# AFNO blocks on one core: the Filter's mixing as 64x64 tiles, two units at once, and softshrink split between VectorE and ScalarE

## The reference

```python
def afno_filter(x, w1, b1, w2, b2):          # x: 2 x 128 x 128 x 128
    xf = rfft2(x, axes=(1, 2), norm='ortho') # 65 columns kept
    xf = xf.reshape(B, H, W // 2 + 1, 8, 16) # 8 blocks of 16 channels
    o1r = relu(xr @ w1[0] - xi @ w1[1] + b1[0])   # per block
    o1i = relu(xi @ w1[0] + xr @ w1[1] + b1[1])
    o2r = softshrink(o1r @ w2[0] - o1i @ w2[1] + b2[0], 0.01)
    o2i = softshrink(o1i @ w2[0] + o1r @ w2[1] + b2[1], 0.01)
    return irfft2(o2r + 1j * o2i) + x

h = afno_filter(layer_norm(x) * n1_g + n1_b, ...) + x
y = gelu(layer_norm(h) @ mw1 + mb1) @ mw2 + mb2 + h
```

## Time and profile before

| | |
|---|---|
| median of 3 runs | 1652.82 us (1651.64 to 1653.29) |
| the profiled execution | 1653.2 us, its span 1651.4 us |
| TensorE busy, granted clock | 1598.6 us (97%), 1.000 |
| VectorE busy | 1076.1 us (65%) |
| ScalarE busy | 938.4 us (57%) |
| GpSimd busy | 619.8 us (38%) |

### The profile page before, as it was taken

The page is one execution under the profiler, slowest core; times in us unless marked ns, Lnnn a source line. Parts: engine busy times, 40 slices in busy tenths (PEclk is TensorE's granted clock), DMA queues, the critical chain, the costliest instruction groups (busy, mean ns, idle before and its releaser), DMA issues.

```text
span 1651.4 us, 34968 instructions
## 1 busy us (share of the span) xinstructions
PE 1598.6 (97%) x11278; PEld 1445.4 (88%) x11278; DVE 1076.1 (65%) x2697; ACT 938.4 (57%) x1782; POOL 619.8 (38%) x774
## 2 busy tenths in 40 slices
PE   0999999999999999999999999999999999999999
PEld 0999988888999988888899998888889998888888
DVE  7889566556559856655656966665664995555453
ACT  5655276666535546666644545666663553666665
POOL 4800046766800016676660002677673000211111
PEclk9999999999999999999999999999999999999999
DMA  7500713333300062333320042333331006011111
GB/s 222 197 15 1 238 45 108 95 102 121 97 14 1 8 236 83 108 95 102 122 78 1 1 166 94 101 108 101 102 110 46 1 1 204 27 32 38 32 39 45
DMA packets 167249, 137.67 MB, mean 83 GB/s; under 512 B 9459, under 2 KB 131189, under 8 KB 167157
## 3 DMA queue, kind: packets, MB, share of 16 engines
q1 hardware_dynamic: 166354, 136.23, 26.1%
q10 hardware_dynamic: 802, 0.21, 0.1%
HBM read 69.29 MB, written 67.11 MB: 83 GB/s over the span
## 4 chain that ended last, share of the span: by engine, by line
PE 79%; DVE 14%; issue 4%; ACT 1%; SPq 1%; DVEq 1%; DMA 1%; POOL 0%; ACTq 0%
PE ps L756 27%; PE ps L558 7%; PE ps L722 7%; PE ps L724 7%; PE ps L683 7%; PE ps L723 7%; DVE vsb L1105 4%; PE ps L716 3%; PE ps L702 3%; PE ps L708 3%; DVE csb L1107 3%; DVE usb L1095 3%; DVE usb L1096 2%; PE ps L568 2%; PE ps L612 2%
## 5 line engine op out<-in xcount | busy, mean ns | idle before, releaser
L756 PEld LDWEIGHTS ps<-mw,gel 128*128 128x128 f32 x4000 | 520.6, 191 | 42.3
L756 PE MATMUL ps<-mw,gel 128*128 128x128 f32 x4000 | 523.7, 274 | 0.0
L875 ACT ACTIVATE gel<-ps,mb1f 128x512 f32<-128x512 f32 x500 | 343.7, 687 | 250.5 <-PE ps L724 219.7
L1460 POOL TENSOR_TENSOR arena<-arena,mb2rep 128x512 f32<-128x512 f32 x125 | 160.1, 1281 | 654.6 <-ACT hn L861 654.6
L722 PE MATMUL ps<-hth,mw1h 128*128 128x512 f32 x512 | 260.3, 508 | 2.9 <-DVE htl L1206 1.5
L1449 POOL TENSOR_SCALAR arena<-xnext,rstd,shift 128x128 f32<-128x128 f32 x360 | 159.3, 462 | 207.6 <-DVE shift L1344 207.6
L861 ACT ACTIVATE hn<-arena,shift,rstd 128x128 f32 (+1 forms) x512 | 221.7, 483 | 16.7 <-DVE shift L1344 16.7
L1189 DVE TENSOR_TENSOR arena<-ps,arena 128x512 f32 (+1 forms) x60 | 41.5, 691 | 252.4 <-PE ps L708 233.8
L724 PE MATMUL ps<-hth,mw1l 128*128 128x512 f32 x512 | 202.1, 395 | 0.0
L723 PE MATMUL ps<-htl,mw1h 128*128 128x512 f32 x512 | 200.8, 392 | 0.0
L846 ACT ACTIVATE osb<-usb,vectors 128x512 f32<-128x512 f32 (+1 forms) x136 | 95.6, 703 | 158.3 <-DVE usb L1096 158.3
(11 more groups left out here) (118 smaller groups left out, 2397.9 us busy)
## 6 DMA issues: line engine op xcount, KB each, us to landing
arena<-aside SPq DMA_DIRECT2D x128, 256.0 KB, 5.0
aside<-gz SPq DMA_DIRECT2D x96, 256.0 KB, 3.0
between<-xout SPq DMA_DIRECT2D x62, 256.0 KB, 2.3
out_dram<-xout SPq DMA_DIRECT2D x62, 256.0 KB, 2.3
xnext<-between SPq DMA_DIRECT2D x60, 256.0 KB, 3.1
aside<-first SPq DMA_DIRECT2D x32, 256.0 KB, 2.3
xnext<-in_x_dram SPq DMA_DIRECT2D x30, 256.0 KB, 3.1
first<-in_x_dram SPq DMA_DIRECT2D x1, 960.0 KB, 7.2
```

What stands on the lines that cost most here:

```text
L756: mm = pe.matmul(ps[:, r % 2, P * i:P * i + P], gel[:, r % 2, m, P * i:P * i + P], mw2[:, s // IMAGES, m, :], start=(m == 0 and i == 0), s ...
L875: act.activation(gel[:, r % 2, m, :], ps[:, 2 + m % 2], ACT.Gelu, bias=mb1f[:, s // IMAGES, m:m + 1]).then_inc(gelu_out, 1)
L1460: pool.tensor_tensor(t, t, b, ALU.add).then_inc(mb2_done, 1)
```

## The change

The mixing works on two units at once, called a pair `p` (units 2p and 2p+1). Each half of 64 channels is cut once more into quarters of 32 channels (QUART), so that real and imaginary part of a quarter fill 64 partitions. `w1s` and `w2s` become 64x64 blocks. A pair's first mixing is 4 matmuls for the even and 4 for the odd part, one in each 64x64 tile of the array. Its second mixing is 16 matmuls with a 64x128 stationary operand, in the upper and the lower half of the array by turns, and writes to two banks per pair, in pairs of banks that alternate. The biases in `b2cols` are raised by LAM, and softshrink becomes min(v, 0) + relu(v - 2 LAM): VectorE adds the bias (`biased`, L1155), ScalarE applies the rectifier (`upper`, L889), VectorE takes the minimum and the sum in one operation (`shrink`, L1172). TensorE's, ScalarE's and VectorE's programs are written in another order for it. The weights come in 12 transfers and the vectors in 4, in place of 3 and 1; for the first layer the vectors move to SyncE's queue, behind the constants. The Nyquist column is no longer copied to a place of its own.

The core of the diff:

```diff
-            def mix2(s, n):
-                q, kws = n % 2, 1 if n in (2, 3) else GROUP
-                pe.wait_ge(o_out, UNITS * s + n + 1)
-                if n >= 2:
-                    pe.wait_ge(v_out, UNITS * s + n - 1)
-                for i in range(kws):
-                    mm = pe.matmul(ps[:, 4 + q, P * i:P * i + P], osb[:, q, i, :],
-                                   w2s[:, q].rearrange("p r c -> p (r c)"), start=True, stop=True)
-                mm.then_inc(m2_mm, 1)
+            def mix1(s, p):
+
+                alone = p == 1
                 if not alone:
-                    pe.wait_ge(g_out, 2 * BATCHES * s + g + 1)
-                if n >= 2:
-                    pe.wait_ge(u_out, UNITS * s + n - 1)
+                    pe.wait_ge(g_out, 2 * BATCHES * s + spectrum_of(2 * p + 1) + 1)
+                if p:
+                    pe.wait_ge(u_out, UNITS * s + 2 * p)
+
+                def quarters(j0, j1, depth, k0, k1, kind, start):
+
+                    for q in range(2):
+                        for g in range(2):
+                            own_rows = slice(HALF * g + depth[0], HALF * g + depth[1])
+                            cols = slice(HALF * (g ^ q), HALF * (g ^ q) + HALF)
...
+                            mm = pe.matmul(dst[:, :, k0:k1], w1s[own_rows, kind, q].rearrange("p r c -> p (r c)"),
+                                           gsb[own_rows, q, j0:j1, k0:k1], start=start, stop=True, skip_group_check=True)
+                    return mm
...
+                elif p:
+                    quarters(0, GROUP, (0, HALF), 0, EVEN, 0, True)
+                    mm = quarters(0, GROUP, (0, HALF), EVEN, P, 1, False)
...
+                mm.then_inc(m1_mm, 2)
+
+            def mix2(s, p):
+                kws = 1 if p == 1 else GROUP
+                if p >= 2:
+                    pe.wait_ge(v_out, UNITS * s + 2 * p - 2)
+                for q in range(2):
+                    pe.wait_ge(o_out, UNITS * s + 2 * p + q + 1)
+                    for i in range(kws):
+                        for g in range(2):
+                            own_rows = slice(HALF * g, HALF * (g + 1))
+                            at_ = 2 * HALF * 2 * q + HALF * i
+                            mm = pe.matmul(ps[:, 4 + 2 * (p % 2) + g, at_:at_ + HALF], osb[own_rows, q, i, :],
+                                           w2s[own_rows, q].rearrange("p r c -> p (r c)"), start=True, stop=True)
+                mm.then_inc(m2_mm, 2)
...
+                for q in range(2):
+                    dft_h(s, 4 + q)
+                for p in range(PAIRED):
+                    if p + 1 < PAIRED:
+                        mix1(s, p + 1)
+                    if p == EDGE_PAIR + 1:
+                        pe.wait_ge(y_done, (UNITS + 1) * s + 2 * EDGE_PAIR + 2)
+                    mix2(s, p)
+                    if p == EDGE_PAIR:
                         edges(s)
+                    if p and p + 2 < PAIRED:
+                        for q in range(2):
+                            dft_h(s, 2 * p + 4 + q)
...
+            def upper(s, n, q, kws=GROUP):
+                act.wait_ge(v_out, UNITS * s + n + 1)
+                act.activation(csb[:, q, :, 0:kws], vsb[:, q, :, 0:kws], ACT.Relu, bias=cut[:, :]).then_inc(c_out, 1)
...
                 def batch(b, last=False):
                     n = 2 * b + 2
-                    g_copy(s, n + 1, 1)
-                    e_copy(s, n, 0)
+                    for q in range(2):
+                        e_copy(s, n + q, q)
                     o_relu(s, n, 0)
-                    if not last:
-                        g_copy(s, n + 2, 0)
-                    e_copy(s, n + 1, 1)
+                    for q in range(2):
+                        upper(s, n - 2 + q, q, kws=1 if isinstance(b, int) and b == 1 else GROUP)
+                        if not last:
+                            g_copy(s, n + 2 + q, q)
                     o_relu(s, n + 1, 1)
...
+            def biased(s, n, q, odd, kws=GROUP):
...
+                dve.tensor_tensor(v, src, bias, ALU.add).then_inc(v_out, 1)
+
             def shrink(s, n, b, q, kws=GROUP):
 
-                dve.wait_ge(m2_mm, UNITS * s + n + 1)
...
-                dve.tensor_tensor(v, src, bias, ALU.add).then_inc(v_out, 1)
-                dve.wait_ge(v_out, UNITS * s + n + 1)
-                own.add(dve.tensor_scalar(cl, v, -LAM, LAM, ALU.max, ALU.min))
-                own.settle()
...
-                dve.tensor_tensor(dst, v, cl, ALU.subtract).then_inc(y_done, 1)
+                dve.scalar_tensor_tensor(dst, v, 0.0, cl, ALU.min, ALU.add).then_inc(y_done, 1)
...
+                def batch(b, odd, last=False):
+                    if not last:
+                        combine(s, 2 * b + 4, 0)
                     for q in range(2):
-                        if not (last and q):
-                            combine(s, 2 * b + 3 + q, 1 - q)
+                        biased(s, 2 * b + 2 + q, q, odd)
+                    if not last:
+                        combine(s, 2 * b + 5, 1)
+                    for q in range(2):
                         shrink(s, 2 * b + 2 + q, b, q)
...
+            load_weights(act, params[0])
```

More of the change, by code:

```diff
@@ L207, in afno @@
         mask = cst[:, 7 * P:].rearrange("p (s b) -> p s b", s=3)
[L208 to L209 removed]
+        w1s = sb("w1s", [P, 2, 2, 2, QUART])
+        w2s = sb("w2s", [P, 2, 2, QUART])
+        swapped = sb("swapped", [P, 3, 2])
+        cut = sb("cut", [P, 1])
         wraw = sb("wraw", [P, 2, 2, 2, BLOCK])
         vectors = sb("vectors", [P, 4, 2])
[L212 removed]
+        b1v, dcbias = vectors[:, 2, :], vectors[:, 3, :]
+        gain64, beta64 = ((vectors[:, i, 0:1], swapped[:, i, 1:2]) for i in range(2))
         b2rep = sb("b2rep", [P, 2, 2, HALF])
@@ L235, in afno @@
         csb = at("csb", [P, 2, HALF, GROUP, 2], o); o += size(csb.shape)
-        nyq = at("nyq", [P, 2, P], o); o += size(nyq.shape)
         yedge = at("yedge", [P, 2, 2, HALF, 2], o); o += size(yedge.shape)
@@ L527, in dc_bias @@
                 for q in range(2):
-                    mm = pe.matmul(ps[:, 7, q:q + 1], w1s[0:HALF, 0, q].rearrange("p r c -> p (r c)"),
-                                   beta64[0:HALF, q:q + 1], start=(q == 0), stop=True, skip_group_check=True)
-                mm.then_inc(dc_mm, 1)
+                    if q:
+                        pe.wait_ge(dc_mm, 2 * n + 1)
+                    for g in range(2):
+                        rows_, cols = slice(HALF * g, HALF * g + QUART), slice(HALF * (g ^ q), HALF * (g ^ q) + HALF)
+                        mm = pe.matmul(ps[cols, 7, q:q + 1], w1s[rows_, 0, q].rearrange("p r c -> p (r c)"),
+                                       beta64[q][rows_], start=(q == 0), stop=True, skip_group_check=True)
+                    mm.then_inc(dc_mm, 1)
             def evicted(s, cg):
@@ L836, in e_copy @@
                 act.wait_ge(m1_mm, UNITS * s + n + 1)
+                if not (isinstance(n, int) and n < 2):
+                    act.wait_ge(o_out, UNITS * s + n - 1)
                 src = ps[:, 2 + q].rearrange("p (j k) -> p j k", j=GROUP)
@@ L907, in _ @@
                 for q in range(2):
-                    with act.Fori(0, CGROUPS // 8) as j:
-                        for r in ((0, 2) if s else range(4)):
-                            a_out(s, q, j, r)
+                    for g in range(2):
+                        with act.Fori(0, CGROUPS // 16) as j:
+                            for r in ((0, 2) if s else range(4)):
+                                a_out(s, q, g, j, r)
                 if s:
@@ L1249, in _ @@
                     for q in range(2):
-                        with dve.Fori(0, CGROUPS // 8) as j:
-                            for r in (1, 3):
-                                a_out(s, q, j, r)
+                        for g in range(2):
+                            with dve.Fori(0, CGROUPS // 16) as j:
+                                for r in (1, 3):
+                                    a_out(s, q, g, j, r)
                         if q == 0 and s % IMAGES == 0:
```

201 lines of the change are left out of this document (107 added, 94 removed).

## The result

The changed kernel takes 1731.55 us (median of 4 runs, 1726.04 to 1737.38), the kernel before 1653.05 us in the same series of runs. The ratio is 1.0476, 95% interval 1.0438 to 1.0515: **slower by 78.5 us**. The profiled execution took 1737.38 us (span 1735.6), so rows of its trace are some 6 us above the median.

The account below looks back on a forecast made before the run. TensorE and VectorE were both taken as full before; afterwards a three-engine chain makes a pair 7.18 us instead of 5.30. 1653.2 + 112.8 (pairs) + 4 (stage ends) + 1 (layer change) = 1771.0 us, range 1690 to 1885.

Parts of the forecast that it names:

- The bound before: Filter's mixing stage before the change: TensorE and VectorE both full, 2.65 us a unit, 5.30 us a pair.
- the new chain: Second mixing's tail, bias addition, rectifier, copy, rectifier, copy, then first mixing: 3.48 us a pair, with TensorE waiting.
- The second mixing: Pair's second mixing: 32 loads, the array's halves loading beside each other, 1.78 us, bound 3.55.
- Rival B: Second mixing: weight loads of the two halves go one by one, 3.55 us; 8.95 a pair, 1877 us; chance 0.23.
- The first mixing: Pair's first mixing: only two records run at a time, never four, so 1.72 us.
- the change of shape: Switch of tile shape between first and second mixing: 0.20 us a pair in the chain, bounds 0 and 0.20.
- rival A: First mixing: all four tiles run together, 0.86 us; 6.32 a pair, 1719 us in all; chance 0.25.
- The clock: TensorE's granted clock falling in its waits: named as a sign of being wrong, adding to any case, no size given.
- The ends: Mixing stage's start and end: longer last VectorE work and first pair's wait, +1 us a step, 4 in all.
- the layer change: Twelve more transfers issued by SP delay the residual loads; VectorE and TensorE lose some time, +1 us.
- Rival D: First mixing's wait for copies: chain does not bind, TensorE's work does; 4.96 us a pair, 1633 us; chance 0.10.

Follow-up runs that it names:

- run 5: Changed kernel with its mixing matmuls issued tile by tile, and the second mixing one half of the array after the other; 1769.86 us, one run.
- run 3: Changed kernel plus 14 spare matmuls of constants per step in TensorE's 3.11 us gap; 1716.79 us, ratio 1.0387 to the kernel before.
- run 2: Changed kernel with TensorE's, ScalarE's and VectorE's programs reordered, transforms of pair p+2 ahead of second mixing p; 1642.5 us, ratio 0.9936 to the kernel before.
- run 4: Changed kernel with softshrink's split undone: clamp back on VectorE, no shrink rectifier on ScalarE; ratio 1.026 to the kernel before.
- run 1: Changed kernel with only ScalarE's order altered: both copies ahead of both rectifiers of the shrink; ratio 1.0494 to the kernel before.
- run 7: The three orders of run 2 plus 9 spare matmuls ahead of each step's last second mixing; 1637.38 us, ratio 0.991 to the kernel before.
- run 8: Changed kernel with ScalarE's order of run 1 and the 14 spare matmuls of run 3; 1710.57 us, ratio 1.0362 to the kernel before.

## Why the prediction was right, and where not

The direction and the range held: slower, 1731.55 us in 1690 to 1885. The forecast was 1771.0, 39 us too much. Point by point:

- **The bound before, and the new chain: right.** TensorE stands before the first mixing, released by ScalarE's copy (1.23 us at 133.58). By my steps, from the second mixing's start to VectorE's 1.78 + 0.28 + 0.04 = 2.10 us (measured 128.38 to 130.51, 2.13), and from there to the first mixing 0.69 + 0.08 + 2.28 + 0.11 = 3.16 (measured 3.07). One thing I had missed: the rectifier into `osb` (130.49), which waits for the same second mixing, stands on ScalarE ahead of the chain's rectifiers; it ends with the bias addition and costs nothing.
- **The second mixing: right.** 32 loads in 1.86 us, the two halves beside each other. Rival B falls.
- **The first mixing: wrong, and this is the step that failed.** I wrote "the next tile's matmul starts only with that second record" and took 1.72 us, with 0.20 for the change of shape. Measured are 1.03 us for both. Four records start together, and run 5 shows it for tile-by-tile issue too. The price was rival A's (0.86 + 0.20 = 1.06), which had a chance of 0.25, and so was its pair, 6.32 against 6.23 measured. The chain of 3.48 us, which the two share, is what held. The Trainium skill's TensorEngine Tiling (Array Packing), "Key Properties", states what rival A took, that different tiles load and multiply in parallel; the rows agree. I had set against it the strict program order of TensorE: Matmul & The Clock Gate, "The mechanism"; that order lets matmuls of different tiles be under way at once, and I read into it that both records of one matmul come before the next matmul's first. The rows show otherwise, and in run 5 the tiles' matmuls do not even start in program order.
- **The clock: named, not priced.** It was in the list of what would make me wrong, with no term in the sum. Run 3 prices the fall behind the 3.11 us gap at 14.8 us; those at the stages' ends are part of the next term.
- **The ends: too low.** +4 us for four steps, and +1 for the layer change; measured 15.7 in the change and 16.9 in run 3, partly at half clock, of which the layer change shows nothing. I had counted VectorE's longer last step and the first pair's wait for both its units, at 1 us a step for both; the second alone is 0.9. I had not counted that the pair makes both last units late together, nor that the matmuls which filled the waits of the last second mixings now stand behind them.
- **Rival D**, the faster side, was right in its mechanism and its condition: with the chain out of the way (run 2) the pair is 4.93 to 5.03, for which it had 4.96. The change itself does not reach that point; its orders keep it from it.

In the prologue ScalarE issues seven transfers more, not six; they are hidden there as forecast, since the first mixing of step 0 starts no later (79.37 us instead of 79.67).

The terms put right: 1771.0, less 60 x (7.18 - 6.23) = 57.0, less 30 x 0.09 = 2.7 for the pairs of 6.14, plus 16.9 - 5.0 = 11.9 for the ends, plus 14.8 for the clock, is 1738. The first mixing put the forecast some 60 us too high, the ends and the clock 27 too low; that the whole is off by only 39 is partly luck. The remaining 6 us lie in the stage's first pairs, for which I counted nothing: by this remainder, the pair of the Nyquist column and the edges take less than the units that they replace (the stage is 46.7 us longer in run 3, where sixty pairs at 6.19 instead of 5.30 would make it 53).

**What stays open.** Why the granted clock comes back after 6.8 us in three steps and only after 37.5 us in step 0, behind the same gap of 3.11 us and with the same work, no run tells apart; run 4, with 34.1 us in step 1, says that it is not tied to step 0. Nor is it shown why the clock fell for longer in run 1, whose pairs wait for less time than those of the change, or whether the waits of 0.97 and 0.71 us at the stages' ends are what lets it fall there. Of the step from 5.69 us a pair (run 1) to 4.93 (run 2), TensorE's, VectorE's and the rest of ScalarE's new order were made together, and no run says what each is worth. The 14 us that run 7 loses at the stages' ends were read from the trace; nothing was tried against them.

## What to carry to other kernels

When a change makes the work of an engine shorter and also reorders it, price the two apart: the same tiles and the same split are 4.8% over the kernel before in the change's order, and 0.9% under it in the order of run 7, with one gap filled. On an engine with a program in fixed order, put the operation that another engine waits for ahead of the one that itself waits; the same rectifier cost 33 us more ahead of a copy that VectorE waited for than behind it. A wait on TensorE can cost more than its own length, since the clock may be at half behind it: to fill the 3.11 us gap won 14.8 us in four steps, though the filling takes as long as the gap. So look at the granted clock by stretch before comparing times, and fill such a gap before judging anything else.

## What the runs showed of the hardware

- Four 64x64 tiles run together on float32: the 16 records of a pair's first mixing take the 1.03 us up to the second mixing, where the same work in 128x128 form took 0.86 for one unit, 1.72 for two. It did not matter whether the tiles were issued by turns or one after the other (1.03 and 1.05 us), and in the second case their matmuls started out of the program's order (run 5).
- Loads of 64x128 in the upper and lower half of the array overlap fully by turns (32 in 1.86 us) and partly one half after the other (2.47 us).
- The granted clock fell to half in or right behind gaps of 3.11 us (the change) and 2.01 us (run 2), and near one of 1.36 us (run 8), while waits of 0.88 to 1.23 us in every pair left it whole between 90 and 160 us in run 3. Yet at the stages' ends of the change and of run 3 it fell too, where the last waits are 0.97 and 0.71 us; the length of a gap alone does not tell. In the change's step 0 it then stayed at half for 37.5 us, with TensorE busy for 12.32 of the 13 us from 97 to 110.
